# An attention layer's finish moved into its last 25 steps, and one-hots made two steps earlier

## What is computed

```python
h = relu(x @ w_in + b_in)
for l in range(3):
    q = h @ wq[l];  k = h @ wk[l];  v = h @ wv[l]
    scores = sum(q[dst] * k[src], axis=1) * scale
    mx = segment_max(scores, dst)
    exp_ = exp(clip(scores - mx[dst], -50, 50))
    alpha = exp_ / (segment_sum(exp_, dst)[dst] + 1e-9)
    agg = segment_sum(v[src] * alpha[:, None], dst)
    h = relu(agg @ wp[l] + bp[l] + h)
x = x + h                                   # then the third network, on relu(layernorm(x)):
edge_nn = lambda s, W, b: relu(relu(s @ W.T + b) @ W.T + b)   # for two relations
```

## Time and profile before

| | us |
|---|---|
| median of 3 runs | 5124.53 (5122.9 to 5125.28) |
| the profiled execution | 5136.45 |
| its span, first to last instruction | 5134.7 |
| last gather of the middle layer begins | 2965.32 |
| last score of that layer begins | 2981.89 |
| its last edge sum is taken | 3007.86 |
| its last block is clipped | 3039.83 |

### The profile page before, as it was taken

The page is one execution under the profiler, slowest core; times in us unless marked ns, Lnnn a source line. Parts: engine busy times, 40 slices in busy tenths (PEclk is TensorE's granted clock), DMA queues, the critical chain, the costliest instruction groups (busy, mean ns, idle before and its releaser), DMA issues.

```text
span 5134.7 us, 55804 instructions
## 1 busy us (share of the span) xinstructions
PE 2274.7 (44%) x12472; PEld 1570.9 (31%) x12472; DVE 2867.5 (56%) x8608; ACT 1029.4 (20%) x2805; POOL 3262.8 (64%) x3348
## 2 busy tenths in 40 slices
PE   3120340005200577778777787777920006971100
PEld 2020230003100455556555565555720003431000
DVE  7754243335443678887788877888634332124433
ACT  1000100001000243334333353333510003430000
POOL 4767677776777467772777737776057773027776
PEclk6565655556555789999999999999965557985555
DMA  5556566665666433332333323333156663236665
GB/s 181 190 172 220 180 200 205 205 199 171 206 206 205 142 110 106 106 106 76 98 105 106 105 75 100 105 104 99 47 193 205 205 206 101 90 139 205 207 205 188
DMA packets 273899, 780.32 MB, mean 152 GB/s; under 512 B 64561, under 2 KB 95794, under 8 KB 269746
## 3 DMA queue, kind: packets, MB, share of 16 engines
q0 software_dynamic: 159984, 437.08, 30.3%
q1 hardware_dynamic: 113602, 339.68, 16.9%
HBM read 459.57 MB, written 316.93 MB: 151 GB/s over the span
## 4 chain that ended last, share of the span: by engine, by line
PE 29%; DVE 10%; POOL 10%; issue 7%; DMA 6%; ACT 1%; DVEq 1%; POOLq 0%; ACTq 0%; SPq 0%
POOL HC L471 10%; PE PS L1219 9%; PE PS L1211 7%; DVE W L1811 4%; PE PS L1145 3%; DMA HC<-table_typ,run_typ 3%; PE PS L927 3%; DMA HC<-table_rel,run_rel 3%; PE PS L1200 2%; DVE HC L1875 2%; DVE work L1819 1%; DVE score L1819 1%; PE PS L921 1%; PE PS L1107 1%; DVE HC L1634 1%
## 5 line engine op out<-in xcount | busy, mean ns | idle before, releaser
L1634 DVE SCALAR_TENSOR_TENSOR HC<-HC,run_rst 128x256 f32<-128x256 f32 x1950 | 946.7, 485 | 1401.0 <-DMA HC<-table,run_max 738.5
L471 POOL DMA_INDIRECT HC<-table,run_max x1173 | 1159.8, 989 | 461.7 <-issue 314.3
L449 POOL DMA_INDIRECT HC<-table,idx_src x648 | 636.1, 982 | 429.1 <-DMA table<-B 207.0
L1049 PE MATMUL PS<-ident,HC 128*128 128x128 f32 x10 | 3.4, 446 | 1608.6 <-DVE HC L1634 1608.6
L449 POOL DMA_INDIRECT X<-table,idx_src x600 | 579.8, 966 | 184.3 <-issue 131.2
L1875 DVE SCALAR_TENSOR_TENSOR HC<-HC,fcol,PS 128x257 f32 x1248 | 592.6, 475 | 156.6 <-PE PS L1219 137.3
L471 POOL DMA_INDIRECT HC<-table_typ,run_typ x391 | 380.6, 973 | 400.7 <-DMA table_typ<-HC 281.8
L1211 PE MATMUL PS<-AM,work 128*128 x3744 | 633.3, 281 | 0.0
L471 POOL DMA_INDIRECT HC<-table_rel,run_rel x391 | 379.0, 969 | 299.1 <-DMA table_rel<-AM 180.2
L1049 PEld LDWEIGHTS PS<-ident,HC 128*128 128x128 f32 x10 | 1.5, 204 | 1611.6 <-DVE HC L1634 1102.5
L1211 PEld LDWEIGHTS PS<-AM,work 128*128 128x128 bf16 x3744 | 373.2, 100 | 171.6 <-issue 5.0
(11 more groups left out here) (254 smaller groups left out, 3878.9 us busy)
## 6 DMA issues: line engine op xcount, KB each, us to landing
prefix<-HC SPq DMA_DIRECT2D x485, 512.0 KB, 3.2
table_typ<-HC SPq DMA_DIRECT2D x19, 1024.0 KB, 3.8
HC<-table,run_max POOLq DMA_INDIRECT x1173, 2.8
HC<-table,idx_src POOLq DMA_INDIRECT x648, 2.8
table<-AM SPq DMA_DIRECT2D x15, 640.0 KB, 3.8
table<-B SPq DMA_DIRECT2D x15, 640.0 KB, 3.4
X<-table,idx_src POOLq DMA_INDIRECT x600, 2.8
table_rel<-AM SPq DMA_DIRECT2D x10, 640.0 KB, 4.4
```

The costliest lines, as they stand in the source:

```text
L449: pool.indirect_dma_start(held(t)[:, 0:D], None, table, bass.IndirectOffsetOnAxis(ap=idx_src[:, t:t + 1], axis=0)).then_inc(landed[t % AHE ...
L471: pool.indirect_dma_start(run_slot(k), None, src, bass.IndirectOffsetOnAxis(ap=run_idx[s[1]][:, j:j + 1], axis=0)).then_inc(landed[k], 16)
L1634: V.scalar_tensor_tensor(run_slot(k), run_slot((j - 1) % SLOTS), run_rst[:, j:j + 1], run_slot(k), fade, join).then_inc(pooled, 1)
```

## The change

It does three things.

First, `make_hots` is called in steps t with t % 4 = 1 for the four steps that begin at t+7, so that each set of one-hots stands two steps earlier in DVE's list; its own wait on ACT's weighing (the ring of 40 one-hots) comes two steps earlier too.

Second, the stage `finish` is gone. The block b of `A2` is complete after step sum 391+b at the latest, so the attention loop does the finish of block b itself, from step t = 424+b on (`WHOLE` = 424): DVE adds the small number and inverts one column (`sum_of` in step 424+b, `invert_sum` one later), PE transposes the unscaled block (`turn_sums`, step 424+b), ACT copies it out (`take_sums`, one step later), PE multiplies by `Wvp` (`project_sums`, two steps later), DVE scales by the reciprocal and adds to `B` in one operation (`add_sums`, four steps later), ACT clips (`clip`, five steps later). The loop has 454 steps instead of 448. ACT's scaling pass and DVE's copy are gone. The PSUM banks are 0 and 1 for the transposes, 2 and 6 for the products.

Third, the beginning of the third network becomes a stage of its own, `relate`, after the last layer.

The diff, cut to its core:

```diff
+WHOLE = TILES + LAG + 1
@@ ACT, attention
+                    def take_sums(b):
+                        act.wait_ge(turned, tu + b + 1)
+                        if b >= 3:
+                            act.wait_ge(mm_done, mm + b - 2)
+                        nc.scalar.activation(agg_cols[:, b % 3, :], PS[:, b % 2, 0:D], ACT.Copy).then_inc(spread, 1)
...
-                    for t in range(STEPS + LAG):
+                    for t in range(WHOLE + BLOCKS + 5):
...
+                        if 0 <= t - WHOLE - 1 < BLOCKS:
+                            take_sums(t - WHOLE - 1)
+                        if 0 <= t - WHOLE - 5 < BLOCKS:
+                            clip(t - WHOLE - 5)
@@ PE, attention
+                    def turn_sums(b):
+                        pe.wait_ge(attend_added, t0 + (TILES + b if b < BLOCKS - 1 else STEPS))
+                        if b == 0:
+                            pe.wait_ge(scored, t0 + STEPS)
+                        if b >= 2:
+                            pe.wait_ge(spread, tu + b - 1)
+                        turn(b % 2, A2[:, b, :]).then_inc(turned, 1)
+                    def project_sums(b):
+                        pe.wait_ge(spread, tu + b + 1)
+                        if b >= 2:
+                            pe.wait_ge(mm_out, oo + b - 1)
+                        else:
+                            pe.wait_ge(hot_in, q0 + STEPS // 4)
+                        dense((2, 6)[b % 2], [agg_cols[:, b % 3, c * P:(c + 1) * P] for c in range(K2)],
+                              [wview["Wvp"][:, c, :] for c in range(K2)]).then_inc(mm_done, 1)
...
-                        if t >= LAG:
+                        if LAG <= t < STEPS + LAG:
                             attend(t - LAG)
+                        if 0 <= t - WHOLE < BLOCKS:
+                            turn_sums(t - WHOLE)
+                        if 0 <= t - WHOLE - 2 < BLOCKS:
+                            project_sums(t - WHOLE - 2)
@@ DVE, attention
+                    def invert_sum(b):
+                        dve.wait_ge(vec, sums_in[b])
+                        inverted[b] = mark(V.reciprocal(rcol[:, b:b + 1], rcol[:, b:b + 1]))
+                    def sum_of(b):
+                        dve.wait_ge(attend_added, t0 + (TILES + b if b < BLOCKS - 1 else STEPS))
+                        sums_in[b] = mark(V.tensor_scalar(rcol[:, b:b + 1], A2[:, b, D:ROW], SM_EPS, None, ALU.add))
+                    def add_sums(b):
+                        dve.wait_ge(vec, inverted[b])
+                        dve.wait_ge(mm_done, mm + b + 1)
+                        V.scalar_tensor_tensor(B[:, b, :], PS[:, (2, 6)[b % 2], 0:D], rcol[:, b:b + 1], B[:, b, :],
+                                               ALU.mult, ALU.add).then_inc(mm_out, 1)
...
-                        if t % 4 == 3 and (t + 5) // 4 < STEPS // 4:
-                            make_hots((t + 5) // 4)
-                        if t >= LAG:
+                        if t % 4 == 1 and (t + 7) // 4 < STEPS // 4:
+                            make_hots((t + 7) // 4)
+                        if LAG <= t < STEPS + LAG:
...
                             take(t - LAG, blocks[t % CHUNK])
+                        if 0 <= t - WHOLE - 1 < BLOCKS:
+                            invert_sum(t - WHOLE - 1)
+                        if 0 <= t - WHOLE < BLOCKS:
+                            sum_of(t - WHOLE)
+                        if 0 <= t - WHOLE - 4 < BLOCKS:
+                            add_sums(t - WHOLE - 4)
@@ PE, relate
+                    for i in range(BLOCKS + 7):
+                        if 0 <= i - 2 < BLOCKS:
+                            b = i - 2
                             pe.wait_ge(centred, c0 + b + 1)
```

More of the change, by code:

```diff
@@ L75, in plan @@
     for layer in range(LAYERS):
-        s += [("project", layer), ("attention", layer), ("finish", layer)]
-    s += [("runs", "rel"), ("runs", "typ")]
+        s += [("project", layer), ("attention", layer)]
+    s += [("relate",), ("runs", "rel"), ("runs", "typ")]
     return s
@@ L84, in made @@
             "project": {"turned": 1, "mm": 1, "out": 1},
-            "finish": {"turned": 1, "mm": 1, "out": 1, "rows": 1}}
+            "attention": {"turned": 1, "mm": 1, "out": 1, "rows": 1},
+            "relate": {"turned2": 1, "centred": 1, "bn": 1}}
     each = dict(each.get(s[0], {}))
-    if s[0] == "finish" and s[1] == LAYERS - 1:
-        each.update(turned2=1, centred=1, bn=1)
     if s[0] == "runs":
@@ L373, in tables @@
         def tables(n):
-            return sum(1 for s in PLAN[:n] if s[0] == "embed" or s[:2] == ("runs", "max") or s[0] == "finish" and s[1] < LAYERS - 1)
+            return sum(1 for s in PLAN[:n] if s[0] == "embed" or s[:2] == ("runs", "max") or s[0] == "attention" and s[1] < LAYERS - 1)
         def columns(k):
@@ L394, in loads @@
         def loads(s):
-            return {"embed": 1, "project": 2, "finish": 5}[s[0]] + (s[1] if s[0] == "project" else 0) if s[0] != "runs" else \
+            return {"embed": 1, "project": 2, "relate": 5}[s[0]] + (s[1] if s[0] == "project" else 0) if s[0] != "runs" else \
                 (1 if s[1] == "max" else 8)
@@ L601, in _ @@
                     else:
+                        sp.wait_ge(attended, LAYERS * STEPS)
                         for k in range(PARTS):
                             sp.dma_start(X[:, TRS * k:TRS * (k + 1), :], stash[:, TRS * k:TRS * (k + 1), :]).then_inc(x_in[k], 16)
[L604 to L609, removed]
+                elif s[0] == "relate":
+                    begin(sp, n)
+                    for i in range(PARTS):
+                        sp.wait_ge(rel_made, TRS * (i + 1))
+                        for r in range(REL2):
+                            to = table_rel[r * NODES:(r + 1) * NODES, :].rearrange("(b p) d -> p b d", p=P)
+                            sp.dma_start(to[:, TRS * i:TRS * (i + 1), :], rel_rows[:, i % 2, :, r, :]).then_inc(rel_tabled[i % 2], 16)
         @block.scalar
@@ L1290, in _ @@
                             last.then_inc(second_done, 1)
-                        if last_layer and 0 <= i - 7 < BLOCKS:
-                            b = i - 7
+                        if 0 <= i - 4 < BLOCKS:
+                            b = i - 4
                             pe.wait_ge(spread2, u0 + b + 1)
```

121 lines of the change are left out of this document (35 added, 86 removed).

## The result

The changed kernel takes 5153.81 us (median of 5 runs, 5146.57 to 5160.02), the kernel before 5124.53. The ratio is 1.0055, 95% interval 1.004 to 1.0069: slower by 29 us, where 18 us less were forecast.

The account below looks back on a forecast made before the run. DVE, delayed by PE's wait for one-hots, trails POOL, which runs almost at its own pace. One-hots -63.6, finish +14.0 +14.0, last layer +17.8 sum to -17.8 us: 5106.7 us, range 5085 to 5142.

Parts of the forecast that it names:

- the distance to the last score: Attention layers, last gather to last score: earlier one-hots would cut it from 16.57 to 3.57 us, 13.0 a layer.
- the wait at gather 48: POOL's wait for edge sum 0, 7.45 us in the middle layer, would fall under 1.5 us.
- What is then saved per layer is the distance ... and POOL's waits: Earlier one-hots in three attention layers: 3 x (13.0 + 8.2) = 63.6 us saved.
- Nothing is added; 312 operations change place: Earlier one-hots: DVE's list is only reordered, so PE finds them made while DVE does two more scores.
- the lower bound of 40 us saved: One-hots, three layers: 40 us saved if the distance closes only by two thirds and the wait by half.
- another wait keeps DVE behind POOL: Attention layers: ACT's weighing or gather landings leave DVE 8 us behind, 31 us saved, 5139 us; chance 0.13 including no gain.
- The round trip: Steps 428 to 447: edge sum, take, addition and product run in turn between PE and DVE, 2.85 us a step.
- the rival of free overlap: Finish steps: products and edge sums overlap at 1.53 us, take 424 to last clip some 39.5 us, 5032 us; chance 0.05.
- The 6 us that earlier weight loads might have given: Finish rounds: weight loads pulled ahead would take up to 0.1 us off each, 6 us over three layers.
- The clock rival: Finish rounds: PE's clock falls, 1.25 us more a round, 5144 us with half low, 5182 with all; chance 0.18.
- `relate` loses the 1.09 us ... in each of 25 rounds: Last layer: without product and transposes, `relate` falls from 130.8 to 103.6 us, PE at 3.73 us a round.
- The signs I named: Profile: one-hot idle a few us, distance 3.5 to 5, takes 2.7 to 3.05, last clip 61 to 68, `relate` 100 to 107.

Follow-up runs that it names:

- add_first: Changed kernel with DVE's addition of a block put ahead of the take in each step; 5864.88 us, 0.9829 to before, on the slower chips.
- best: Changed kernel with one-hots ahead of the score behind the tile wait, addition ahead of the take, `relate`'s root behind bias and ReLU; 5027.9 us, 0.9823 to before.

## Why the prediction was wrong

**What bounds the kernel.** Right in its reading: the distance to the last score and the wait at gather 48 both went as forecast, and DVE now waits for tiles (108 us).

**"What is then saved per layer is the distance ... and POOL's waits"** is the step of the prediction that failed first. The distance was sized well (13.6 us a layer for 13.0). The waits went too, 26.9 us in three layers, but first to last gather didn't get shorter (+3.7 us for the -24.6 forecast): I took the length of a gather from the trace as a constant. Part of it, 21.5 us, was already the one-hots' doing in before, and moving them without asking what POOL does at that moment raised it to 59.5. "Nothing is added; 312 operations change place" was wrong for that reason, and so was the lower bound of 40 us saved: 37 came. The range was too narrow even by my own numbers: it gave the one-hots +12 us for the worst case, where the bound of 40 us saved, against 63.6, is +24. No rival had this mechanism; the nearest in time, the one in which another wait keeps DVE behind POOL (5139 us), had the wrong cause.

**The round trip.** Right in its order, its place and its size, 2.84 us for 2.85; add_first and best show that the order alone makes it, and the rival of free overlap (39.5 us) is what one gets with the addition ahead of the take: 39.4. The 6 us that earlier weight loads might have given did not come, as the row of 2999.40 shows. The clock rival is refuted: the granted clock was 1.00 in 2980 to 3029, and in the same stretch of the other two layers.

**The last layer.** The step "`relate` loses the 1.09 us ... in each of 25 rounds" was mis-sized: 103.6 us forecast, 115.4 measured. I took 3.73 us a round from PE's own work, and had not followed ACT's order, in which the root waits for DVE ahead of PE's next release. best has the 3.73 us and 106.3 us. Of the 12 us missed, 7 are that order, 4.7 in the rounds and 2.5 at the start; 1.9 go with PE's lower clock at the start; the last 2.7 best has as well, and they stay unexplained.

**The signs I named.** PE's idle time before the transposes of one-hots is 80.7 us, not a few, and 123.0 more stand before the transposes that close a softmax, for DVE; neither costs anything while POOL bounds. Gather 48 (0.30 us), the takes, the clock and 65.3 us to the last clip (61 to 68) came as named. The distance was 2.96, 3.83 and 2.99 us, two of them under the 3.5 named, and `relate` (100 to 107) was 115.4.

The sum on the first chips closes by single parts: -36 us from the one-hots alone and +59 from the finish alone (0.9929 and 1.0116 of 5124.5), +23 together, against +29 with an interval from +20.

## What to carry to other kernels

Before moving a DVE operation in a kernel whose GpSimd queue bounds, lay the two timelines side by side and see what the operation covers: an instruction's length on another engine can be a result of the schedule, as that of the gathers here, and need not be a constant. Where two engines in order hand work to each other in both directions in one step, put the operation that frees the other engine ahead of the one that waits for it; here that order alone is worth 26 us a layer, and makes of a finish that costs 14 us one that saves 11. When a fused loop is cut in two, walk each engine's list in the part that is left for waits that the removed work had covered.

## What was unexpected of the hardware

A gather issued by GpSimd, 0.945 us when undisturbed, stands still when a DVE operation with two tensors in SBUF began more than 0.1 us before it and still runs 0.11 us after its start, until that operation's end: 595 times out of 595, by 0.46 us in the mean where the end lay 0.6 us after the gather's start, and 60 us of the changed kernel in all. The same comparison in four short operations with one tensor hardly holds it (8 us). Sets that began after a gather's start behaved unevenly: most held nothing, a few held it for 0.8 us. And two kinds of chips gave opposite signs for the same change, 1.0055 and 0.9915. On one of them POOL bounds (1.28 us a step); on the other it doesn't (1.51 us), and PE and ACT pause for several us without a cause that the profile shows.
